# A mixture-of-experts block with top-96 gathering: the last four experts of the last tile as two blocks of two

## The reference

```
pe = softmax(posembed @ pos_w + pos_b)
y = moe_mlp(hidden_states, sg_w, su_w, sd_w)
for i in range(E):
    gate_feature = hidden_states * pe[i] @ gate_w + gate_b
    gate_weight, gate_idx = top_k(gate_feature, K)
    gate_weight = softmax(gate_weight)
    gathered = take_along_axis(hidden_states, gate_idx)
    y = y + moe_mlp(gathered * gate_weight, eg_w[i], eu_w[i], ed_w[i])
return silu(layernorm(y) @ m1_w + m1_b) @ m2_w + m2_b
```

## Time and profile before

| what | value |
|---|---|
| three executions | 2891.42, 2885.01, 2889.93 us; median 2889.93 |
| profiled execution, span | 2885.7 us; its own device time is not listed apart |
| PE, DVE, ACT, POOL busy over the span | 83%, 89%, 58%, 57% |
| chain that ended last | DVE 83% |
| block 55, first lookup to first lookup of block 56 | 2777.80 to 2816.80 us |
| last instruction of DVE | starts at 2799.75 us |
| block 56, first lookup to the end of the last put | 2816.80 to 2849.40 us |
| tail | 2849.40 to 2885.7 us |

### The profile page before, as it was taken

The page is one execution under the profiler, slowest core; times in us unless marked ns, Lnnn a source line. Parts: engine busy times, 40 slices in busy tenths (PEclk is TensorE's granted clock), DMA queues, the critical chain, the costliest instruction groups (busy, mean ns, idle before and its releaser), DMA issues.

```text
span 2885.7 us, 55510 instructions
## 1 busy us (share of the span) xinstructions
PE 2387.0 (83%) x12314; PEld 1570.8 (54%) x12314; DVE 2573.7 (89%) x13628; ACT 1678.4 (58%) x3895; POOL 1656.4 (57%) x2118
## 2 busy tenths in 40 slices
PE   4999559998888878887888878888888788889787
PEld 3777336655555555555555555555555555555455
DVE  2454599999999999999999999999999999999980
ACT  1333234776666666665666656666666666666664
POOL 0111034776667666666666766666666666667675
PEclk9899678999999999999999999999999999999997
DMA  3001310111111111010110110111110110110110
GB/s 96 25 26 46 96 22 12 26 28 25 21 25 26 18 28 28 14 29 21 23 28 15 31 24 16 27 25 21 25 28 16 28 28 14 30 26 15 25 23 5
DMA packets 159257, 78.07 MB, mean 27 GB/s; under 512 B 105911, under 2 KB 156204, under 8 KB 156876
## 3 DMA queue, kind: packets, MB, share of 16 engines
q1 hardware_dynamic: 158156, 72.39, 12.3%
q0 software_dynamic: 704, 1.39, 0.1%
HBM read 39.04 MB, written 27.77 MB: 23 GB/s over the span
## 4 chain that ended last, share of the span: by engine, by line
DVE 83%; issue 2%; PE 2%; ACT 1%; POOL 0%; DVEq 0%; DMA 0%; POOLq 0%; ACTq 0%
DVE idx L871 29%; DVE keys L873 28%; DVE vals L867 24%; DVE digits L847 0%; PE ps L1243 0%; DVE digits L846 0%; PE ps L1205 0%; PE ps L1260 0%; DVE keys_rest L873 0%; PE ps L1181 0%; ACT code L926 0%; DVE ntop L842 0%; PE ps L1196 0%; DVEq L676 0%; ACT gu_s L968 0%
## 5 line engine op out<-in xcount | busy, mean ns | idle before, releaser
L871 DVE FIND_INDEX8 idx<-vals,keys 128x8 uint16<-128x192 f32 x2688 | 939.1, 350 | 0.0
L1101 POOL TENSOR_TENSOR picked<-looked_s,code 128x384 f32<-128x384 f32 (+1 forms) x912 | 810.0, 904 | 76.3 <-ACT looked_s L937 68.9
L926 ACT ACTIVATE code<-ps 128x768 bf16<-128x768 f32 (+1 forms) x912 | 735.5, 806 | 186.0 <-PE ps L1181 169.4
L867 DVE MAX8 vals<-keys 128x8 f32<-128x192 f32 x2688 | 817.5, 345 | 28.9 <-issue 28.9
L873 DVE MATCH_REPLACE8 keys<-vals,keys 128x192 f32<-128x192 f32 x2464 | 840.1, 341 | 0.0
L1181 PE MATMUL ps<-rows,codew 128*128 128x384 bf16 (+1 forms) x1824 | 468.2, 339 | 387.2 <-ACT code L926 357.8
L1205 PE MATMUL ps<-picked,place 128*128 128x384 f32 (+1 forms) x1824 | 754.1, 501 | 0.0
L1196 PE MATMUL ps<-code,table 128*128 128x384 bf16 (+1 forms) x2736 | 614.0, 334 | 30.3 <-issue 30.3
L937 ACT ACTIVATE looked_s<-ps 128x384 f32<-128x384 f32 (+1 forms) x912 | 445.5, 489 | 127.0 <-PE ps L1196 124.2
L1181 PEld LDWEIGHTS ps<-rows,codew 128*128 128x128 bf16 x1824 | 149.8, 99 | 606.4 <-ACT code L926 519.8
L1196 PEld LDWEIGHTS ps<-code,table 128*128 128x128 bf16 x2736 | 273.8, 101 | 275.0 <-issue 145.4
(11 more groups left out here) (139 smaller groups left out, 2521.3 us busy)
## 6 DMA issues: line engine op xcount, KB each, us to landing
digit_d<-dcode SPq DMA_DIRECT2D x56, 384.0 KB, 2.6
rows<-digit_d SPq DMA_DIRECT2D x112, 192.0 KB, 4.7
table<-parts SPq DMA_DIRECT2D x240, 9.0 KB
rows<-fill SPq DMA_DIRECT2D x1, 3072.0 KB
wexp<-in_w_exp SPq DMA_DIRECT2D x1, 2304.0 KB
wdown<-in_w_down SPq DMA_DIRECT2D x1, 2304.0 KB
hr<-norm_d SPq DMA_DIRECT2D x120, 12.0 KB
patch<-in_patches SPq DMA_DIRECT2D x16, 108.0 KB, 2.0
```

Of the source, the lines that this page charges most:

```text
L867: nc.vector.max(vals[:, par, e, at], from_keys[:, e, :]).then_inc(chain, 1)
L871: found = nc.vector.max_index(idx[:, par, e, at], vals[:, par, e, at], from_keys[:, e, :])
L926: nc.scalar.activation(code[:, o % 4, :, 0:w], ps[:, CODE_B:CODE_B + 2, 0:w], ACT.Relu).then_inc(code_ready, 1)
L1101: nc.gpsimd.tensor_tensor(picked[:, o % 4, w], looked_s[:, o % 4, w], code[:, o % 4, 1, w], ALU.mult).then_inc(picked_ready, 1)
```

## The change

The last block of the last tile becomes two. `slots` runs a fifth slot for tile 14 (g = 4). `LAST` is the number of the last block, now 57; `halved(n)` is true for the blocks 56 and 57, and `experts_of` gives 2 for them, so that all widths of these two slots are 192 columns. Block 56 now holds experts 12 and 13, block 57 holds 14 and 15. VectorE sorts the same four lists in the same order, but closes block 56 in the first round of block 57. Slot 56 still carries the four units of block 55 at the spots 3, 6, 9 and 12. Slot 57 carries the two units of block 56 at the spots 3 and 8, and the tail the two units of block 57. Blocks up to 55 are as before. Lines behind the change stand 6 to 15 further down.

```
+LAST = BPT * TILES + 1
...
+def half_units(part):
+
+    return [(2 + EXPERTS - 4 + j, EXPERTS - 4 + j, None) for j in range(2 * part, 2 * part + 2)]
...
-        for g in range(BPT):
+        for g in range(BPT + 1):
             slot(TILES, g, True)
...
-        return isinstance(n, int) and n == BPT * TILES
+        return isinstance(n, int) and n == LAST
+
+    def halved(n):
+        return isinstance(n, int) and n >= LAST - 1
...
+        if g == BPT:
+            return pairs_before(t, g - 1) + 1
...
-        return BANDS if isinstance(n, int) and n == 0 else GRP
+        return BANDS if isinstance(n, int) and n == 0 else GRP // 2 if halved(n) else GRP
...
     def mlps(t, g):
 
+        if g == BPT:
+            return t, half_units(0), [3, 8]
...
-                last = 1 if many > 2 else 0
+                last = 1 if many > 2 or last_block(n) else 0
...
-                from_keys = keys_rest if is_rest(t) else keys[:, g]
+                from_keys = keys_rest if is_rest(t) else keys[:, BPT - 1, 2:4] if g == BPT else keys[:, g]
...
-                    chain = chains[pair]
+                    chain = chains[1 if last_block(n) else pair]
...
-                    if o > PREPARE and o - PREPARE <= GRP and not last_block(n):
+                    if o > PREPARE and not last_block(n) and o - PREPARE <= experts_of(n + 1):
...
-            turned_out(BPT * TILES)
-            for u, e, half in units_of(BPT - 1):
+            turned_out(LAST)
+            for u, e, half in half_units(1):
                 activate(TILES, u, e)
...
-            turn_x(BPT * TILES, TILES, 3)
-            last_units = units_of(BPT - 1)
+            turn_x(LAST, TILES, BPT)
+            last_units = half_units(1)
```

More of the change, by code:

```diff
@@ L1222, in up @@
                     pe.wait_ge(xwt_ready, 1)
+                elif e == EXPERTS - 2 and last_tile(tm):
+                    pe.wait_ge(xwt_ready, LAST + 1)
                 elif e is not None and (e % GRP == 0):
@@ L1242, in up @@
                             at = a * D + c * HALF
-                            ins = nc.tensor.matmul(dst, wexp[:, e, at:at + HALF], xwt[:, e % GRP, :], start=True, stop=True)
+                            ins = nc.tensor.matmul(dst, wexp[:, e, at:at + HALF], xwt[:, e % (GRP // 2 if last_tile(tm) and e >= EXPERTS - GRP else GRP), :], start=True, stop=True)
                 ins.then_inc(gate_up, 1)
```

## The result

| | change | before |
|---|---|---|
| median of 12 executions each | 2893.07 us | 2889.29 us |
| their range | 2889.87 to 2897.67 | 2883.71 to 2893.63 |
| ratio, 95% interval | 1.0018 (1.0011 to 1.0026) | |
| span of the profiled execution | 2896.0 us | 2885.7 us |

The change costs 3.8 us, 0.18%. The interval lies above 1, so the cost is real; the ratio itself is within the 0.2% that the prediction calls no difference, and its interval reaches 0.26%. The prediction had 2893.5 us. That it lies within 0.5 us of the median is closer than such a sum can be trusted to: the executions of the change spread over 7.8 us.

The account below looks back on a forecast made before the run. DVE's sorting bounds up to slot 55's stall, PE the gathering after, and the tail is a file of short operations. -2.0 + 13.7 - 8.1 = +3.6 us on the median 2889.93 gives 2893.5 us, range 2885.5 to 2900.5.

Parts of the forecast that it names:

- slot 55: In slot 55 ACT no longer waits for the sort at step 8: -2.0 us, between 0 and 3.3 gained.
- slot 56: Four units at half the columns: 4.6 to the first `up`, four rings of 5.0, seam 1.4; 26.0 us, between 24.8 and 29.
- slot 57: The new slot with two units and two rings of 5.0: 20.3 us, between 17.8 and 22.
- both against the one slot before: Slots 56 and 57 together take 46.3 us where one took 32.6: +13.7, between +10 and +18.4.
- tail: After the last put, two units instead of four (6.7 us less) and half-size entry (1.4 less): -8.1, between -7 and -9.
- the ring: Halved slots: `up`, ACT, POOL's products, `down`, next `up` take 5.0 us whatever the columns, and bound three steps.
- PE's own 3.9: Halved slots: PE's own work in three steps with a unit at 192 columns, 3.9 us.
- Digits of block 57: Taken at step 8 of slot 56: 8.7 us needed, about 11 covered, some 2.3 to spare, no wait.
- Half for half: Rival: half the columns cost half, both slots 32.6 plus 3.1 us for two units; -7.0, 2882.9 us; chance 0.08.
- Longer rings: Rival: each of six rings costs 0.6 us more; +7.2, 2897.1 us; rings and entries at upper end, chance 0.24.
- The clock: Rival: rows over about 2 us late at the seam, slot 57 at half clock; +13.8, 2903.7 us; chance 0.06.
- both halved slots would be cold: By the skill's rule on matmul bursts between transfer waits, both halved slots start at the lower clock; small chance.

Follow-up runs that it names:

- e1: The change with `up` of the next unit ahead of `down` of the last one in the two halved slots; 2892.84 us.
- e2: The change with POOL's three products of each unit in the halved slots on only 16 of 128 tokens, output incomplete; 2889.92 us.
- e6: The change with units of blocks 55 to 57 on VectorE and two alternating banks for raw codes in the halved slots; 2884.53 us, 0.998 of the kernel before.
- e3: The change with the digits of block 57 taken at step 13 of slot 56 instead of step 8; 2901.33 us.
- e4: The change with raw codes of the halved slots alternating between two banks, both halves of a code sharing one; 2894.89 us.
- e8: The change with matmuls nobody reads put into PE's gaps from the last lookup to the end; 2889.35 us, 1.0002 of the kernel before.
- e10: The unsplit kernel before with units of the last two blocks on VectorE and unread matmuls in the tail; 2876.61 us, 0.9962 of the kernel before.
- e9: The change with units of the last three blocks on VectorE, two raw-code banks and unread matmuls in the tail; 2878.87 us, 0.9972 of the kernel before.
- e12: Repeat of e9, the split kernel with all three edits; 2877.41 us, 0.9959 of the kernel before.
- e11: Repeat of e10, the unsplit kernel with units on VectorE and unread matmuls in the tail; 2880.61 us, 0.9974 of the kernel before.

## Why the prediction was right

| term | predicted | measured |
|---|---|---|
| slot 55 | -2.0 | -1.98 (37.02 us) |
| slot 56 | 26.0 us | 26.71 |
| slot 57 | 20.3 us | 20.33 |
| both against the one slot before | +13.7 | +14.44 |
| tail | -8.1 | -8.44 |
| sum | +3.6 | +4.0 by the trace, +3.8 by the medians |

The bound that the forecast turned on was right, and shown: e1 and e2 remove the ring in two ways, and the ups move together at once. The errors of the terms are small and of both signs, which is why the sum is better than its terms.

*Slot 55.* ACT's 3.25 us are gone and 1.98 came through, but by other parts than assumed. From the third to the fourth `up` PE gains 1.71 us (8.91 to 7.20): its first wait behind the stall is gone, the second stays at 1.12 us instead of 1.58, where the prediction left 0.6 for both. The other 0.25 us is the seam, whose two codes are already of 192 columns. That the two add up to 2.0 is in part luck. PE's timeline of the change:

```profile
2809.78 0.50 PE L1194 MATMUL ps<-rows,codew 128*128 128x384 bf16 x2 [1.12 <-ACT code L939]
```

*The ring.* "`up` after `up` at 5.0 instead of 6.17" is 5.15. The part up to POOL's product was right (4.33, measured 4.34); the miss is behind it: 0.66 was taken for `down` from a row where it did not wait. One that waits takes 0.76 to the next `up` (2835.33 to 2836.09), and begins 0.05 behind the product. Times four rings that is 0.6 of slot 56's 0.7 us; slot 57 came out right because its two longer rings met shorter ends.

*The tail.* -8.44 against -8.1, with the fall of the clock alone worth some 0.6 either way. By parts: last put to first `up` 2.28 us instead of 3.99 (-1.7, predicted -1.4), from there to the end of the last `down` 9.65 instead of 16.70 (-7.05, predicted -6.7), and the rest, said to be unchanged, 15.93 instead of 15.61 (+0.3).

*PE's own 3.9.* Confirmed by e6, 3.82 to 3.91. The prediction said of the ring that it takes over as the bound; it did not say that the round through ACT, 0.92 without a unit, grows to a bound of 4.7 in three steps with one, 0.45 below the ring. Whoever removes the ring alone gets 4.70 per unit, not 3.9 (e2; in e1, with the other order, the three spacings rise from 4.07 to 4.61). This doesn't enter the sum, but it is the part of the picture that was missing: the two bounds lie 0.45 us apart, and the sum came out because the larger of them was the one that was counted.

*Digits of block 57.* No wait, as said: in e3, where PE waits for the rows, it goes on 3.86 us after SyncE's issue of them (2844.29 to 2848.15). By that 9.0 us are needed here (2834.30 to 2839.42, and 3.86) against 8.7 predicted; the cover is 12.1 (2834.30 to 2846.37) against 11, so 3.1 us to spare, not 2.3. The price without cover is the full one, as said (e3). The smaller pieces took 2.1 and 3.3 us, as in the earlier trace rows.

*The rivals.* Half for half: wrong for this kernel, nearly right for PE alone (e6). With both bounds gone the two slots cost 38.04, and 32.6 plus two units (3.06) is 35.7; the 2.4 left over are the second seam (1.36 us, 2839.85 to 2841.21) and, by count, the steps' 0.77 instead of 0.73. Longer rings: 0.15 each, not 0.6. The clock: it stayed at 1.00 to the last put, and in e3 it came back within the first steps of slot 57. The assumption that failed there is "slot 57 runs at half the clock": it was taken from the tail, which does stay at 1.2 GHz, and doesn't carry over to a slot. The condition "more than about 2 us" was read from one row, and other rows don't bear it out as a rule: in e3 the clock fell 1.4 us behind PE's last product, while in the kernel before it read 1.00 from 384 to 387 us, with PE busy 0.03 of these 3 us. The Trainium skill ("TensorE: Matmul & The Clock Gate", HAM oscillation) would have every burst after a transfer's wait start at the lower clock. That is what e3's row of 0.50 at 2848 to 2852 shows, for one burst, and the profile of the change has no such wait. So the page's case, bursts between waits for transfers, is not that of the halved slots, whose waits are short and for ACT and POOL; "both halved slots would be cold" was more than it says. In e3 the steps after 2854 are at full clock.

## What to carry to other kernels

A step's parts shrink with its width, its rings (through another engine, a semaphore, back) don't: before splitting work, lay the longest ring beside the busy time that the narrower step will have. When removing one bound gives less than was read off, look for a second one right behind it and remove both (0.8 and 6.4 us alone, 9.0 together, by the slots of one trace each). And ask what an engine that has finished could take over: here moving the units to it and keeping PE's clock up gave 6 to 11 us, where moving the work in time cost 3.8 us by itself and, with the rest in place, gave nothing that the times can show.

## What the runs showed of the hardware

- TensorE's clock fell to 1.2 GHz 1.4 us into a wait of 6.52 us and was back at 2.4 GHz some 5 us after work had begun again (e3, 2848.15 to 2853.2). In the tail of the change it fell and did not come back (0.50 in every window of 4 us from 2872 to 2896); its first two windows:

```profile
2868.00:2872.00 4.00, 2.11 (x11) 1.50 (x10) 0.00 (x0) 0.95 (x3) 0.59 (x1) 0.85 0.02 4
2872.00:2876.00 4.00, 2.67 (x11) 2.22 (x11) 0.00 (x0) 1.73 (x4) 2.16 (x3) 0.50 0.00 0
```

  Where it falls behind the last put differs from run to run of the same tail, 2.3 to 4.7 us (e1 to e4), and the tail's length with it, 28.2 to 26.95 us. Unread matmuls in the gaps held it at 1.00 up to PE's last product and made the tail 3.8 to 5.8 us shorter (e8 to e10).
- A `down` that follows a wait takes 0.76 us to the next instruction, one that doesn't 0.66.
- POOL takes 0.72 us for a product of 96x256 f32 from SBUF, VectorE 0.42 with one operand in PSUM (e6).
- Executions of programs that are alike so far differ by some 4 to 6 us before the stage in question (clock 0.87 or 0.91 from 100 to 200 us, in the attention). Marks inside one trace repeat within 0.3 us where the clock is held (e9 and e12, e10 and e11).
